# One over the root of the variance: a power on GpSimd in place of Newton steps on VectorE, at nine norms

## The reference

```python
def _layernorm(x, axis=-1, eps=1e-05):
    m = jnp.mean(x, axis=axis, keepdims=True)
    v = jnp.var(x, axis=axis, keepdims=True)
    return (x - m) / jnp.sqrt(v + eps)

x = x + jnp.tanh(g_xattn[0]) * _L0_xattn_ref(_layernorm(x, axis=-1), ctx_768, ctx_768, ...)
x = x + jnp.tanh(g_ffn[0]) * _L0_ffn_ref(_layernorm(x, axis=-1), ...)
x = x + jnp.tanh(g_xattn[1]) * _L1_xattn_ref(_layernorm(x, axis=-1), ctx_768, ...)
x = x + jnp.tanh(g_ffn[1]) * _L1_ffn_ref(_layernorm(x, axis=-1), ...)
...
```

## Time and profile before

| | us |
|---|---|
| median of 3 runs | 877.82 |
| lowest, highest | 877.34, 879.37 |
| the profiled execution, its own time | 876.44 |
| its span in the trace | 874.5 |

### The profile page before, as it was taken

How to read it: one execution, slowest core, us unless ns; L and a number is a source line. 1 busy time by engine, 2 the same in 40 slices (tenths; PEclk the granted TensorE clock), 3 DMA queues, 4 the chain that set the end, 5 groups by cost and what they waited for, 6 DMA issues and landing times.

```text
span 874.5 us, 17943 instructions
## 1 busy us (share of the span) xinstructions
PE 605.7 (69%) x5443; PEld 472.7 (54%) x5446; DVE 549.1 (63%) x2108; ACT 354.5 (41%) x896; POOL 242.7 (28%) x285
## 2 busy tenths in 40 slices
PE   1963747877999986998510299916998562299990
PEld 0741326756999974665410288804665452188870
DVE  4887986878677775888650166645888550055552
ACT  0653747832444433555200155503565221144440
POOL 4610000000000004442027455534442017434442
PEclk9985657957999996999855599966999755599996
DMA  5133023000000000000001222250000043222214
GB/s 147 27 117 170 1 67 94 1 7 7 19 24 18 18 0 1 3 2 4 1 14 56 58 72 76 60 158 1 3 3 2 1 113 104 57 53 60 61 40 154
DMA packets 47756, 40.97 MB, mean 47 GB/s; under 512 B 12350, under 2 KB 42332, under 8 KB 47420
## 3 DMA queue, kind: packets, MB, share of 16 engines
q1 hardware_dynamic: 43132, 30.41, 12.2%
q0 software_dynamic: 4544, 9.54, 3.2%
HBM read 23.95 MB, written 15.98 MB: 46 GB/s over the span
## 4 chain that ended last, share of the span: by engine, by line
PE 51%; DVE 21%; POOL 7%; issue 7%; ACT 5%; DMA 3%; SPq 0%; DVEq 0%; ACTq 0%; POOLq 0%
PE ps L1490 10%; PE ps L1060 7%; POOL expert_rows L1559 7%; PE ps L1500 5%; DVE rinvT L479 3%; PE ps L1510 2%; PE ps L653 2%; PE ps L715 2%; PE ps L644 2%; ACT probT L575 2%; PE ps L670 2%; PE ps L1010 2%; PE ps L1079 2%; PE ps L1077 2%; PE ps L1078 2%
## 5 line engine op out<-in xcount | busy, mean ns | idle before, releaser
L1564 POOL DMA_INDIRECT expert_results<-space,b_to x78 | 74.6, 957 | 106.3 <-DVE b_to L1371 101.5
L568 POOL TENSOR_SCALAR xn<-x,moments,rstd 128x128 f32<-128x128 f32 x32 | 25.4, 793 | 278.1 <-DVE rstd L559 278.1
L1490 PE MATMUL ps<-w_block,space 128*128 x312 | 99.9, 444 | 0.0
L1217 DVE SCALAR_TENSOR_TENSOR x<-ps,ew,x 128x128 f32<-128x128 f32 x272 | 76.4, 343 | 28.1 <-PE ps L1060 24.9
L1559 POOL DMA_INDIRECT expert_rows<-sent,slot x64 | 61.7, 963 | 102.2 <-DVE slot L1353 83.3
L1375 DVE TENSOR_TENSOR space<-sg,ps 128x256 f32<-128x256 f32 (+1 forms) x78 | 36.8, 471 | 68.1 <-ACT sg L1430 66.7
L1474 PE MATMUL ps<-const,space 128*128 128x128 f32 x78 | 22.7, 291 | 79.1 <-DMA space<-expert_rows 78.0
L1060 PE MATMUL ps<-w_dn,space 128*128 128x128 f32 x544 | 73.7, 284 | 4.5 <-DVE space L1233 4.3
L1060 PEld LDWEIGHTS ps<-w_dn,space 128*128 128x128 f32 x544 | 69.8, 195 | 10.2 <-DVE space L1233 5.3
L1366 DVE SCALAR_TENSOR_TENSOR b_pick<-space,owner_f 128x4 f32<-128x4 f32 x78 | 16.7, 214 | 86.0 <-DMA space<-expert_rows 86.0
L1490 PEld LDWEIGHTS ps<-w_block,space 128*128 128x128 f32 x312 | 54.8, 196 | 15.5 <-issue 1.6
(11 more groups left out here) (262 smaller groups left out, 1533.8 us busy)
## 6 DMA issues: line engine op xcount, KB each, us to landing
expert_rows<-w_block SPq DMA_DIRECT2D x2, 2632.5 KB, 11.2
space<-expert_rows SPq DMA_DIRECT2D x78, 67.5 KB, 1.9
x_split<-expert_results SPq DMA_DIRECT2D x16, 256.0 KB, 5.1
w_block<-in_L_ffn_w_dram SPq DMA_DIRECT2D x2, 1024.0 KB, 7.0
space<-in_L_ffn_w_dram SPq DMA_DIRECT2D x32, 64.0 KB, 1.9
space<-in_L_ffn_W_dram SPq DMA_DIRECT2D x32, 64.0 KB, 2.3
space<-in_L_ffn_W_dram SPq DMA_DIRECT2D x8, 176.0 KB, 2.8
expert_results<-space,b_to POOLq DMA_INDIRECT x78
```

The source lines that it names most:

```text
L1217: last = dve.scalar_tensor_tensor(x[:, t, :], ps[:, BANK_Y[g % 2], P * j:P * j + P], ew[:, t, bass.ds(n.n, 1)], x[:, t, :], ALU.mult, ALU.add)
L1490: last = pe.matmul(ps[:, bank[s % 2], 0:W], b_xT[:, s % 2, :], w_up[:, bass.ds(expert[s], 1), W * k:W * k + W].rearrange("p a n -> p (a n) ...
L1564: pool.indirect_dma_start(B.results, to, b_y[:, b % 4, :], None).then_inc(y_stored[b % 4], 16)
```

## The change

norm_roots now only aggregates and then asks: its last instruction raises moments_ready, and VectorE waits for roots_ready (ask_roots). GpSimd waits for moments_ready, adds epsilon (a tensor_scalar into var), waits for that through var_ready, and raises var to the power of a tile filled with -0.5 (a tensor_tensor with the power as its operation) into rstd, and raises roots_ready (pool_roots). Nine calls of pool_roots stand in GpSimd's list; later_pool now stands behind the second of them. The tile of -0.5 is set once after setup_pool. att_pool in layers 2 and 3 waits for roots_ready at its new counts. For layer 1's second norm L418 itself carries the signal.

```diff
--- before.py
+++ after.py
@@ -124,9 +124,8 @@
         stats = sb("stats", [P, 2, TILES, 6])
         moments = sb("moments", [P, 3, TILES, 2])
         rstd = sb("rstd", [P, 3, TILES])
-        nr_a = sb("nr_a", [P, 3, TILES])
-        nr_i = sb("nr_i", [P, 3, TILES], I32)
-        nr_t = sb("nr_t", [P, 3, TILES])
+        var = sb("var", [P, 3, TILES])
+        minus_half = sb("minus_half", [P, 3, TILES])
         xn = sb("xn", [P, 2, P])
         xnn = sb("xnn", [P, 2, P])
         inT = sb("inT", [P, 2, 2, P])
@@ -250,7 +249,8 @@
         qk_copied, v_copied = sem("qk_copied"), sem("v_copied")
         scored, top_ready, centered, exped = sem("scored"), sem("top_ready"), sem("centered"), sem("exped")
         p_turned, p_copied_act = sem("p_turned"), sem("p_copied_act")
-        roots_ready, k_spread = sem("roots_ready"), sem("k_spread")
+        var_ready, half_ready = sem("var_ready"), sem("half_ready")
+        moments_ready, roots_ready, k_spread = sem("moments_ready"), sem("roots_ready"), sem("k_spread")
         attended, sum_inverted, normed = sem("attended"), sem("sum_inverted"), sem("normed")
         o_turned, o_copied, y_done = sem("o_turned"), sem("o_copied"), sem("y_done")
         x_done = sem("x_done")
@@ -377,7 +377,7 @@
             def body(at):
                 if (i := at(0)) is not None:
 
-                    pool.wait_ge(roots_ready, A.L - 1)
+                    pool.wait_ge(roots_ready, 2 * A.L + 2)
                     free_again(pool, in_turned, A.base, i, 2)
                     norm_tile(pool, A.sub, i)
                 if (i := at(2)) is not None:
@@ -404,10 +404,10 @@
                     norm_roots(dve, 0)
                 elif A.L == 2:
                     dve.wait_ge(moe_stats, 4)
-                    norm_roots(dve, 0, done=(roots_ready, 1))
+                    norm_roots(dve, 0)
                 else:
                     combine(dve, BLOCK[2])
-                    norm_roots(dve, 0, done=(roots_ready, 2))
+                    norm_roots(dve, 0)
             dve.wait_ge(row_done, A.L + 1)
             dve.tensor_scalar(bias_row[:, :], ps[:, 7, 0:P], gates[:, A.L:A.L + 1], None, ALU.mult).then_inc(row_copied, 1)
             dve.wait_ge(row_copied, A.L + 1)
@@ -415,8 +415,7 @@
 
                 second = moments[:, 2, :, 1]
                 linked_ln(dve, dve.tensor_tensor(second, moments[:, 0, :, 1], rstd[:, 0, :], ALU.mult))
-                linked_ln(dve, dve.tensor_tensor(second, second, rstd[:, 0, :], ALU.mult))
-                norm_roots(dve, 2)
+                ask_roots(dve, dve.tensor_tensor(second, second, rstd[:, 0, :], ALU.mult))
                 linked_ln(dve, dve.tensor_tensor(rstd[:, 2, :], rstd[:, 2, :], rstd[:, 0, :], ALU.mult))
 
             def body(at):
@@ -533,35 +532,28 @@
                 ins = dve.bn_stats(stats[:, 0, t, :], src[:, t, :])
             linked_ln(dve, ins)
 
-        def norm_roots(dve, first, last=None, done=None):
-
-
-
+        asked = [0]
+
+        def norm_roots(dve, first, last=None):
 
             last = first if last is None else last
-
-            def linked(ins):
-                linked_ln(dve, ins)
-            for n in range(first, min(last, 1) + 1):
+            for n in range(first, last + 1):
                 for t in range(TILES):
                     ins = dve.bn_aggr(moments[:, n, t, :], stats[:, n, t, :])
-            if first < 2:
-                linked(ins)
-            some = slice(first, last + 1)
-            root, var, half, guess = rstd[:, some, :], nr_a[:, some, :], nr_t[:, some, :], nr_i[:, some, :]
-            linked(dve.tensor_scalar(var, moments[:, some, :, 1], EPS, None, ALU.add))
-
-            linked(dve.tensor_scalar(guess, var.bitcast(I32), 1, None, ALU.arith_shift_right))
-            linked(dve.tensor_scalar(root.bitcast(I32), guess, -1.0, float(0x5F3759DF), ALU.mult, ALU.add))
-            for n in range(3):
-                linked(dve.tensor_tensor(half, var, root, ALU.mult))
-                linked(dve.scalar_tensor_tensor(half, half, -0.5, root, ALU.mult, ALU.mult))
-                ins = dve.scalar_tensor_tensor(root, half, 1.5, root, ALU.add, ALU.mult)
-                if n < 2 or not done:
-                    linked(ins)
-            if done:
-                ins.then_inc(done[0], 1)
-                dve.wait_ge(done[0], done[1])
+            ask_roots(dve, ins)
+
+        def ask_roots(dve, ins, wait=True):
+            asked[0] += 1
+            ins.then_inc(moments_ready, 1)
+            if wait:
+                dve.wait_ge(roots_ready, asked[0])
+
+        def pool_roots(pool, count, first, last=None):
+            some = slice(first, (first if last is None else last) + 1)
+            pool.wait_ge(moments_ready, count)
+            pool.tensor_scalar(var[:, some, :], moments[:, some, :, 1], EPS, None, ALU.add).then_inc(var_ready, 1)
+            pool.wait_ge(var_ready, count)
+            pool.tensor_tensor(rstd[:, some, :], var[:, some, :], minus_half[:, some, :], ALU.pow).then_inc(roots_ready, 1)
 
         def norm_tile(eng, sub, i):
 
@@ -1701,10 +1693,19 @@
         @block.gpsimd
         def _(pool):
             setup_pool(pool)
+            pool.memset(minus_half[:, :, :], -0.5).then_inc(half_ready, 1)
+            pool.wait_ge(half_ready, 1)
+            pool_roots(pool, 1, 0)
             qff_round_weights(pool)
+            pool_roots(pool, 2, 0, 1)
             later_pool(pool)
+            pool_roots(pool, 3, 0)
+            pool_roots(pool, 4, 2)
+            pool_roots(pool, 5, 0)
             for L in (2, 3):
+                pool_roots(pool, 2 * L + 2, 0)
                 att_pool(pool, ATT[L])
+                pool_roots(pool, 2 * L + 3, 0)
                 blocks_pool(pool, BLOCK[L])
 
         @block.scalar
```

## The result

The changed kernel takes 890.37 us in the median against 877.58 of the kernel before in the same comparison, 1.016 times as long, with a 95% interval from 1.012 to 1.0201. The profiled execution took 890.26 us, its span is 887.5, 13.0 more than the 874.5 of before. So the change is slower, by about what the rival of a slow power gave (888.4), and outside the range that I drew.

What follows compares the result with a forecast made beforehand. Bound by VectorE's serial Newton instructions at eight exposed norms: removing them and adding GpSimd's work gains 5.9 us, less 0.3 for later_pool, net 5.6; from the median, 872.2 us forecast, range 864.5 to 888.5.

Steps and rivals of the forecast that it cites:

- later_pool: GpSimd block moved behind the 32-wide root, now wholly beside L800 on VectorE: collision costs 0.3 us, bounds 0 and 2.4.
- rival of a slow power: At the eight exposed norms, GpSimd's power as a long per-element routine outlasts the twelve steps: 888.4 us at 2.9; chance 0.27.
- p: Duration of GpSimd's power on 16 columns, not in the trace: 1.1 us, between 0.285 and 4.4.
- my own formula: Gain over the eight norms on the path before the later_pool term: 15.8 - 9p us, 5.9 at p = 1.1.
- eight exposed norms: All norms but the first lie on the path: five of 2.54 us, two of 2.61, one of 2.70; 20.6 in all.
- the chain's 0.21 us for each instruction: VectorE's Newton instructions at each norm run one after another, 0.21 us apart, each waiting for the last.
- fixed terms: Per 16-wide norm, add and signals between engines beside the power: 0.63 us at five norms, 0.65 at two.
- the add: GpSimd's epsilon add at each norm, 128x16, priced from L1668: 0.37 us.
- hidden norm: The first norm, in setup, is covered by the weight DMA that L773 awaits: 4.25 us of cover, power up to 3.6.
- first-call load: Rival: the first power, in setup, loads code; decides from 2.5 us, 874.7 us at twice that; chance 0.04.
- The clock of PE: Rival: after a norm, TensorE's clock rises sooner or later, 2.9 us either way in one stage, 869.3 or 875.1; chance 0.06.
- a measurement can tell 0.2% here: For the whole kernel's time, a measurement can tell about 0.2%, 1.8 us, from no change.

Runs made afterwards that it cites:

- e1: The changed kernel with a plain product in place of the power, same engine, shapes and semaphores: 861.29 us, 0.9827 of the kernel before.
- e5: The kernel before with two Newton steps instead of three, on VectorE: 865.3 us, ratio 0.9858 to the kernel before.
- after: The profiled execution of the changed kernel, roots by GpSimd's power in place of VectorE's Newton steps: 890.26 us.
- e2: The changed kernel with later_pool held by one wait until VectorE is through with its run over xn_all: 887.6 us, 1.0121 of the kernel before.
- e11: The kernel before with two Newton steps instead of three, measured again on another chip: 872.33 us, 0.9932 of the kernel before.
- e7: The kernel before with two Newton steps instead of three and later_pool held until VectorE is through with xn_all: 869.86 us against 874.97, ratio 0.9934.

## Why the prediction was wrong, step by step

**The step that failed is the price of the power.** I bounded p by 0.285 and 4.4 and took the middle on a ratio scale, 1.1, with no row near it. It is 2.93: 2.7 times that, and inside the bounds. With it my own formula gives 15.8 - 9 x 2.93 = -10.6, the number that stood under the slow power. That rival's mechanism was right, with one word to mend: the routine is long per column, not per element, since 1 partition costs what 128 do. What I held against it, that sixteen elements are few, was worth nothing, because 157 ns for a column against a product's 2 is a factor of about 75. The reason for it, that no row shows POOL at anything but plain arithmetic, was the better one: an operation without a row should have left the two signs about equal, and the range should have reached past p = 2.9.

**The form of the sum held.** Exposure against p is one for one (e1), none of the eight exposed norms was covered by other work, and the chain's 0.21 us for each instruction is confirmed by e5. The fixed terms were a little too dear: the add took 0.264 us instead of 0.37 (the row that I went by, L1668, was a long one: the same instruction takes 0.27 to 0.28 in eleven of the other twelve traces), so a 16-wide norm has p + 0.45 (3.38 - 2.93), where I had p + 0.63.

**The hidden norm stayed hidden,** as p was below the 3.6 that it could bear: idle 0.72 us before L765. There was no first-call load: the first power took 2.94 us and started 0.08 us behind its add, the others took 2.93. The 6 us that the Trainium skill, GPSIMD Engine Reference, section 2.1, states for a first call aren't seen here.

**later_pool was mis-sized and its mechanism misread.** I took 0.3 us, going by an L800 that ran beside a tensor_scalar of POOL. Measured are 1.30 between the two traces and 1.46 between after and e2. The row to go by was the memset of 1.80 us in the earlier trace rows: of the six instructions only it holds L792 up by more than 0.1 us, and it does so until it ends. The Trainium skill, SBUF — State Buffer, section "SBUF: two separate sides", says that GpSimd and a VectorE operation in a two-port mode take turns at a shared pair of ports, the first holding it for its whole instruction, and that an operation with two SBUF inputs is shut out only by one of GpSimd that reads SBUF. The memset reads nothing; the tensor_scalars (L792, L555, L554) wait it out and the tensor_tensor and scalar_tensor_tensor beside it don't, which agrees if the tensor_scalars run in a two-port mode; no row shows the mode. But by the same rule POOL's tensor_scalars of 0.60 to 0.73 us (value_bias) should hold L792 up too, until they end. They don't: beside them L792 takes 410 ns at most. The two L792 beside the memset (1861 and 1668 ns instead of about 340, overlapping) make 1.3 us of the 1.4 between the 5.64 us for the sixteen in after and the 4.2 in e2.

In the setup the rows go both ways: the L568 of 732 ns runs from 24.21 to 24.94 and ends just behind POOL's 23.36 + 1.50 = 24.86, and three more do likewise (608 to 728 ns), while others run wholly beside a POOL tensor_scalar in 330 to 347 ns. So the wait for a memset is shown; when a POOL tensor_scalar holds VectorE up stays open.

The fixed terms that were too dear and later_pool that was too cheap nearly cancel: without later_pool the measured stretches are 9.15 us longer, where the formula has 10.6, and with it 10.45, where it has 10.9.

**The clock of PE** I priced at 2.9 us a stage and gave it a chance of 0.06. The price holds for the group (6.84 against 3.91); the worst stage differs by 5.4 us. But it isn't a rival of the power: it comes and goes between executions of one code, up or down (in the two traces of the kernel before, two and none of the three gate groups run at 1.2 GHz; in those of the changed kernel, two and one). What it spoils is the other sentence, that a measurement can tell 0.2% here. Intervals from ten to twelve runs are 0.3 to 0.4% to each side, and from four or five runs 0.4 to 0.6%.

## What to carry to other kernels

When a short chain is moved to another engine, the exposure is easy to sum and the one unknown is how long that engine takes for the one new operation; if no row shows that operation, measure it alone at two widths before believing any middle of its bounds. A special function on GpSimd can be a routine per column: at 16 columns (2.93 us) it cost more than twelve dependent VectorE instructions (2.54), at one column it takes 0.55. And of a block of POOL work that is moved, look for its longest memset and for the VectorE tensor_scalars that will stand beside it.

## What was not expected of the hardware

- GpSimd's power takes about 0.39 us and 0.157 for each column up to 32, on 1, 16, 64 and 128 partitions alike, and nearly the same on 1.7, 1.0 and 0.0003.
- A tensor_scalar of VectorE that meets GpSimd's memset of 1.80 us ends with it or up to 0.15 us behind it: 1861, 1853, 1748, 1839, 1902 and 1944 ns in after, e1, e5, e11, e2 and e7, instead of 180 to 343; a tensor_tensor beside the same memset takes 192.
- The granted clock behind a norm stays at 0.50 or rises to 1.00 in executions of the same code, 6.84 against 3.91 us for 32 matmuls, and the time differs by 12.7 us between the fastest and the slowest of 28 runs.
